# Gate projected channel by token, value sums and their denominators made in channel-by-token layout

## What is computed

```python
xn = layernorm(x)                                  # (16, 128, 64)
q, k, v = xn @ Wq, xn @ Wk, xn @ Wv                # 8 heads of 16 channels
attn = softmax(q @ k.T / 4)                        # per row and head, 128 x 128
out = (attn @ v) * sigmoid(xn @ Wg + bg)           # (16, 128, 128)
t = x + out @ Wo + bo
```

## Time and profile before

| | |
|---|---|
| median of 3 runs | 94.19 us (94.04 to 95.80) |
| the profiled execution | 94.28 us, of which the span of the profile is 92.5 us |
| TensorE | busy 75.1 us of the span (81%) |
| VectorE | busy 65.5 us (71%) |
| ScalarE | busy 63.1 us (68%) |
| GpSimd | busy 60.1 us (65%) |
| maxima, first and last row | start at 14.28 and 57.83 us |
| last row of `t_all` | starts at 66.84 us |
| granted TensorE clock | 0.969 of full speed, mean over the span |

### The profile page before, as it was taken

The page is one execution under the profiler, slowest core; times in us unless marked ns, Lnnn a source line. Parts: engine busy times, 40 slices in busy tenths (PEclk is TensorE's granted clock), DMA queues, the critical chain, the costliest instruction groups (busy, mean ns, idle before and its releaser), DMA issues.

```text
span 92.5 us, 2812 instructions
## 1 busy us (share of the span) xinstructions
PE 75.1 (81%) x928; PEld 51.3 (55%) x928; DVE 65.5 (71%) x246; ACT 63.1 (68%) x153; POOL 60.1 (65%) x112
## 2 busy tenths in 40 slices
PE   1988777699899999999999969898798949998000
PEld 1625444266575666566557556576586718997000
DVE  0657377865978887877797868845995576789850
ACT  4247649569979999999999957663335773578120
POOL 5851969841894764835899572647739576948950
PEclk9999999999999999999999999999999999999755
DMA  2768255567146426553355953000000000001103
GB/s 61 180 221 317 77 98 102 113 120 113 32 92 95 96 39 120 117 100 61 73 113 113 63 115 56 11 4 0 0 0 7 0 0 0 0 0 62 59 4 113
DMA packets 18862, 6.82 MB, mean 74 GB/s; under 512 B 17248, under 2 KB 18272, under 8 KB 18848
## 3 DMA queue, kind: packets, MB, share of 16 engines
q1 hardware_dynamic: 18480, 6.27, 33.1%
q10 hardware_dynamic: 368, 0.36, 1.6%
HBM read 1.91 MB, written 0.52 MB: 26 GB/s over the span
## 4 chain that ended last, share of the span: by engine, by line
PE 30%; DVE 19%; POOL 14%; issue 13%; ACT 13%; DMA 5%; DVEq 1%; POOLq 1%; ACTq 0%
PE bank L1045 5%; DMA qk_t<-stack 5%; DVE stack L531 5%; POOL rstd L943 4%; PE banks L1100 4%; PE banks L1105 3%; POOL stack L846 3%; ACT prob L364 3%; PE bank L1055 3%; ACT zn L452 2%; PE bank L1205 2%; PE bank L1019 2%; ACT stack L341 2%; PE banks L1004 2%; DVE xn L508 2%
## 5 line engine op out<-in xcount | busy, mean ns | idle before, releaser
L531 DVE TENSOR_REDUCE stack<-banks 128x8 f16<-128x1024 f32 x16 | 19.4, 1210 | 0.4 <-PE banks L1004 0.4
L364 ACT ACTIVATE prob<-banks 128x1024 f32<-128x1024 f32 x16 | 16.6, 1038 | 1.1 <-PE banks L1031 1.1
L846 POOL TENSOR_TENSOR stack<-qkg,stack 128x256 f16<-128x256 f32 x16 | 11.1, 694 | 8.4 <-ACT qkg L343 8.1
L856 POOL TENSOR_TENSOR og<-og,rden 128x128 f32<-128x128 f32 x16 | 6.4, 403 | 8.5 <-DVE og L549 8.5
L539 DVE COPY q_t<-bank 128x512 f16<-128x512 f16 x16 | 6.8, 424 | 7.3 <-PE bank L1019 7.3
L1045 PE MATMUL bank<-prob,v_aug 128*32 128x128 f32 x256 | 10.3, 279 | 0.6 <-ACT prob L364 0.6
L341 ACT ACTIVATE stack<-bank 128x512 f16<-128x512 f32 x16 | 9.6, 600 | 0.8 <-PE bank L993 0.8
L372 ACT ACTIVATE u_sb<-bank 128x256 f32<-128x256 f32 x16 | 6.3, 394 | 5.5 <-PE bank L1045 5.2
L784 POOL TENSOR_TENSOR rstd<-rstd,neg_half 128x4 f32<-128x4 f32 (+1 forms) x9 | 8.3, 920 | 0.8
L1105 PE MATMUL banks<-ones,ident 128*128 128x256 f16 x53 | 7.4, 273 | 1.5 <-DVE stack L531 1.5
L343 ACT ACTIVATE qkg<-bank 128x384 f32<-128x384 f32 x16 | 8.0, 500 | 0.0
(11 more groups left out here) (132 smaller groups left out, 185.6 us busy)
## 6 DMA issues: line engine op xcount, KB each, us to landing
w_in<-in_w SPq DMA_DIRECT2D x1, 512.0 KB, 5.6
out<-res SPq DMA_DIRECT2D x3, 128.0 KB, 1.9
x_all<-in_x SPq DMA_DIRECT2D x2, 128.0 KB, 2.5
x_all<-in_x SPq DMA_DIRECT2D x1, 256.0 KB, 3.2
w_in<-in_w SPq DMA_DIRECT2D x1, 256.0 KB, 5.8
b_b<-in_b SPq DMA_DIRECT2D x1, 256.0 KB, 6.0
qk_t<-stack SPq DMA_TRANSPOSE x16, 3.1
vectors_b<-in_vectors ACTq DMA_DIRECT2D x1, 160.0 KB, 3.5
```

What stands on the lines that cost most here:

```text
L364: nc.scalar.activation(prob[:, s % 2], s2_both_p, ACT.Exp, scale=HD ** -0.5).then_inc(exp_done, 1)
L531: nc.vector.tensor_reduce(q[:, :, :, SHIFT], s1_both_p, AX, ALU.max, negate=True).then_inc(max_done, 1)
L846: nc.gpsimd.tensor_tensor(stack_slots(b, 2, 0), qkg[:, b, 0:2 * INNER].rearrange("t (a h c) -> t a h c", a=2, h=HEADS), stack_slots(b, 0, ...
```

## The change

The value sums are no longer turned back to token by channel; everything up to Wo stays channel by token.

- **project** streams 384 columns (q, k, v) instead of 512, and two further matmuls hold the gate's 128 columns of w_hi and w_lo as weights and stream the row's tokens, so the gate comes out channel by token. ACT takes its tanh from PSUM with the bias (a column, halved once on DVE) as an operand. gate_input, gates and `gate` go.
- **values** sums two heads into the same 32 output channels: v_aug of the first holds [v, 0], of the second [0, v]. 8 more matmuls of the same shape with `twos` (2.0 or 0) as weights give each channel its denominator. Both outputs are 128 x 128.
- outputs, transpose_outputs, transpose_gated and gated go. gate_outputs reads both from PSUM: the reciprocal is now over 128 x 128 denominators. divide multiplies 128 x 128 by 128 x 128, and its output is project_out's weights.
- project_out and residual come one step earlier (OUT_LATE 6 to 5), STEPS is ROWS+6 instead of ROWS+9, and what follows on DVE, POOL and PE moves one step up. In the last steps PE runs shifted_scores ahead of values, and DVE runs copy_q ahead of gate_outputs.
- The turned q uses one bank throughout; the last row's values go to the projection's bank. Fillers shrink a little.

```diff
-Q_FREE = 13
-S1_LATE, Q_LATE, U_LATE, GATED_LATE, OUT_LATE = 2, 3, 4, 5, 6
-UT_LATE = 4
+STEPS = ROWS + 6
+
+
+S1_LATE, Q_LATE, U_LATE, OUT_LATE = 2, 3, 4, 5
...
-        u_p = bank[B_U][:, 0:2 * TOK].rearrange("c (a q) -> c a q", a=2)
-        ut_p = bank[B_UT][:, 0:2 * TOK].rearrange("q (h c) -> q h c", h=HEADS)
-        y_p = bank[B_U][:, 2 * TOK:2 * TOK + DIM]
+        u_p = [bank[b][:, 0:TOK] for b in (B_U, B_PROJ)]
+        den_p = [bank[b][:, TOK:2 * TOK] for b in (B_U, B_PROJ)]
+        y_p = bank[B_TURN][:, 0:DIM]
...
-                    act.wait_ge(gate_ok, s - 3)
                     act.wait_ge(tq2_done, s - 3)
-                qk = proj_p[:, 0:2 * INNER].rearrange("t (a h c) -> t a h c", a=2, h=HEADS)
-                nc.scalar.activation(stack_twice(b), qk.unsqueeze(3).broadcast_to([TOK, 2, HEADS, 2, HD]), ACT.Copy,
+                both = proj_p[:, 0:2 * INNER].rearrange("t (a h c) -> t a h c", a=2, h=HEADS)
+                nc.scalar.activation(stack_twice(b), both.unsqueeze(3).broadcast_to([TOK, 2, HEADS, 2, HD]), ACT.Copy,
                                      scale=1 / WSCALE)
-                nc.scalar.activation(qkg[:, b, :], proj_p[:, 0:3 * INNER], ACT.Copy,
-                                     scale=1 / WSCALE).then_inc(qkg_ok, 1)
+                nc.scalar.activation(qk[:, b, :], proj_p[:, 0:2 * INNER], ACT.Copy,
+                                     scale=1 / WSCALE).then_inc(qk_ok, 1)
                 if s >= V_BUFS:
                     act.wait_ge(pv_done, s - V_BUFS + 1)
-                nc.scalar.activation(v_aug[:, s % V_BUFS, :, 0:HD],
-                                     proj_p[:, 3 * INNER:4 * INNER].rearrange("t (h c) -> t h c", h=HEADS),
-                                     ACT.Copy, scale=1 / WSCALE).then_inc(proj_copied, 1)
-
-            def gates(s):
-
-                b = s % 4
-                act.wait_ge(gate_ok, s + 2)
-                if s >= 4:
-                    act.wait_ge(ut_read, s - 2)
-                nc.scalar.activation(th[:, b:b + 2, :], gate[:, b:b + 2, :], ACT.Tanh, scale=0.5).then_inc(tanh_done, 1)
+                nc.scalar.activation(value_slots(s % V_BUFS),
+                                     proj_p[:, 2 * INNER:3 * INNER].rearrange("t (p a c) -> t p a c", p=4, a=2),
+                                     ACT.Copy, scale=1 / WSCALE)
+                if s == 0:
+                    act.wait_ge(bg_ok, 1)
+                if s >= V_BUFS:
+                    act.wait_ge(u_read, s - V_BUFS + 1)
+                nc.scalar.activation(th[:, s % V_BUFS, :], proj_p[:, 3 * INNER:4 * INNER], ACT.Tanh, bias=bg_half[:, 0:1],
+                                     scale=0.5 / WSCALE).then_inc(proj_copied, 1)
...
-            def outputs(s):
-
-                b = s % 2
-                act.wait_ge(pv_done, s + 1)
-                if s >= 2:
-                    act.wait_ge(ut_done, s - 1)
-                nc.scalar.activation(u_sb[:, b], u_p, ACT.Copy).then_inc(u_copied, 1)
-
-            def gated(s):
-
-                b = s % 2
-                act.wait_ge(ogt_done, s + 1)
-                if s >= 2:
-                    act.wait_ge(wo_done, s - 1)
-                nc.scalar.activation(og_t[:, b, :], ogt_p, ACT.Copy).then_inc(ogt_copied, 1)
...
             def gate_outputs(s):
 
                 b = s % 4
-                dve.wait_ge(ut_done, s + 1)
-                dve.wait_ge(tanh_done, s // 2 + 1)
+                dve.wait_ge(pv_done, s + 1)
                 if s >= 4:
                     dve.wait_ge(og_ok, s - 3)
-                nc.vector.reciprocal(rden[:, b, :], ut_p[:, :, HD])
-                nc.vector.scalar_tensor_tensor(out=og1[:, b, :].rearrange("t (h c) -> t h c", h=HEADS),
-                                               in0=th[:, b, :].rearrange("t (h c) -> t h c", h=HEADS), scalar=1.0,
-                                               in1=ut_p[:, :, 0:HD], op0=ALU.add, op1=ALU.mult).then_inc(ut_read, 1)
+                nc.vector.reciprocal(rden[:, b, :], den_p[s // (ROWS - 1)])
+                dve.wait_ge(proj_copied, s + 1)
+                nc.vector.scalar_tensor_tensor(out=og1[:, b, :], in0=th[:, s % V_BUFS, :], scalar=1.0, in1=u_p[s // (ROWS - 1)],
+                                               op0=ALU.add, op1=ALU.mult).then_inc(u_read, 1)
...
+                if t >= ROWS+1 and live(t - S1_LATE):
+                    copy_q(t - S1_LATE)
+                if live(t - U_LATE):
+                    gate_outputs(t - U_LATE)
                 if live(t - OUT_LATE):
                     residual(t - OUT_LATE)
-                if live(t - S1_LATE):
+                if t < ROWS+1 and live(t - S1_LATE):
...
-            def gate_input(s):
+            def low(s):
+
                 b = s % 4
-                pool.wait_ge(qkg_ok, s + 1)
+                pool.wait_ge(qk_ok, s + 1)
+                nc.gpsimd.tensor_tensor(stack_slots(b, 2, 0),
+                                        qk[:, b, :].rearrange("t (a h c) -> t a h c", a=2, h=HEADS),
+                                        stack_slots(b, 0, 1), ALU.subtract).then_inc(split_ok, 1)
+
+            def divide(s):
+
+                b = s % 4
+                pool.wait_ge(u_read, s + 1)
                 if s >= 4:
-                    pool.wait_ge(tanh_done, (s - 4) // 2 + 1)
-                nc.gpsimd.tensor_tensor(gate[:, b, :], qkg[:, b, 2 * INNER:3 * INNER], bg_b, ALU.add).then_inc(gate_ok, 1)
...
+                nc.gpsimd.tensor_tensor(og[:, b, :], og1[:, b, :], rden[:, b, :], ALU.mult).then_inc(og_ok, 1)
...
-                nc.tensor.matmul(proj_p, x_t[:, s, :], w_hi[:, :], start=True, stop=False)
+                nc.tensor.matmul(proj_p[:, 0:3 * INNER], x_t[:, s, :], w_hi[:, 0:3 * INNER], start=True, stop=False)
                 if s == 0:
                     pe.wait_ge(w_lo_ok, 1)
-                nc.tensor.matmul(proj_p, x_t[:, s, :], w_lo[:, :], start=False, stop=True).then_inc(proj_done, 1)
+                nc.tensor.matmul(proj_p[:, 0:3 * INNER], x_t[:, s, :], w_lo[:, 0:3 * INNER], start=False, stop=True)
+                nc.tensor.matmul(proj_p[:, 3 * INNER:4 * INNER], w_hi[:, 3 * INNER:4 * INNER], x_t[:, s, :],
+                                 start=True, stop=False)
+                nc.tensor.matmul(proj_p[:, 3 * INNER:4 * INNER], w_lo[:, 3 * INNER:4 * INNER], x_t[:, s, :],
+                                 start=False, stop=True).then_inc(proj_done, 1)
...
-                drained("u", u_copied)
-                drained("y", t_ok)
+                if s == ROWS - 1:
+                    pe.wait_ge(proj_copied, ROWS)
+                else:
+                    drained("u", u_read)
+                if s == 0:
+                    pe.wait_ge(twos_ok, 3)
                 issued["u"] += 1
-                for a in range(2):
-                    for p in range(4):
-                        last = nc.tensor.matmul(u_p[32 * p:32 * p + 32, a, :], v_aug[:, b, 2 * p + a, :],
-                                                prob[:, s % 2, a, p, :], start=True, stop=True)
+                for what in range(2):
+                    target = (u_p, den_p)[what][s // (ROWS - 1)]
+                    for a in range(2):
+                        for p in range(4):
+                            columns = (v_aug[:, b, 2 * p + a, :], twos[:, VCOLS * a:VCOLS * (a + 1)])[what]
+                            last = nc.tensor.matmul(target[32 * p:32 * p + 32, :], columns, prob[:, s % 2, a, p, :],
+                                                    start=a == 0, stop=a == 1)
                 last.then_inc(pv_done, 1)
-
-            def transpose_outputs(s):
-                pe.wait_ge(u_copied, s + 1)
-                drained("turned", ut_read)
-                drained("q", tq2_copied)
-                issued["turned"] += 1
-                for a in range(2):
-                    last = nc.tensor.transpose(ut_p.rearrange("q (p a) c -> q p a c", a=2)[:, :, a, :],
-                                               u_sb[:, s % 2, a, :], ident[:, :])
-                last.then_inc(ut_done, 1)
-
-            def transpose_gated(s):
-                pe.wait_ge(og_ok, s + 1)
-                drained("gated", ogt_copied)
-                drained("x", x_t_ok)
-                issued["gated"] += 1
-                nc.tensor.transpose(ogt_p, og[:, s % 4, :], ident[:, :]).then_inc(ogt_done, 1)
 
             def project_out(s):
                 if s == 0:
                     pe.wait_ge(ld["columns"], 16)
-                pe.wait_ge(ogt_copied, s + 1)
-                drained("u", u_copied)
+                pe.wait_ge(og_ok, s + 1)
+                drained("x", x_t_ok)
                 drained("y", t_ok)
                 issued["y"] += 1
-                nc.tensor.matmul(y_p, og_t[:, s % 2, :], wo, start=True, stop=True).then_inc(wo_done, 1)
+                nc.tensor.matmul(y_p, og[:, s % 4, :], wo, start=True, stop=True).then_inc(wo_done, 1)
...
+                if t >= ROWS and live(t - Q_LATE):
```

(7 more changed lines are left out.)

144 lines of the change are left out of this document (63 added, 81 removed).

## The result

The changed kernel is slower. Its median is 100.72 us (99.59 to 101.07, four runs), beside 95.0 us for the kernel before on the same chip (94.04 to 96.21, four runs); the ratio is 1.068, with a 95% interval of 1.053 to 1.083. The ratio compares only the undisturbed executions of both kernels, so it is not the quotient of the two medians. The forecast was 97.4 us with a range of 95.0 to 100.0: the direction was right, the time lies outside the range, and the loss is 5.7 us where 3.2 were forecast (97.4 against the 94.19 shown).

A forecast was written before the change was run, and what follows sets the result against it. VectorE was to bind at 3.05 us a step. Start -0.7, middle +3.4 and tail +0.2 gave +2.9 on 94.28, so 97.2 us, put at 97.4 for small waits; range 95.0 to 100.0.

The forecast's parts named there:

- the middle: Stretch from row 3's maxima to row 15's, twelve steps: forecast 37.3 us against 33.94, +3.4.
- Behind it nothing is changed: From the last row of t_all to the end: no change in time, 0 us.
- VectorE becomes the bound: VectorE's step grows from 2.08 to 3.05 us, above TensorE's 2.79.
- I therefore take the upper slope: ... 1180 ns: VectorE's reciprocal of 128 elements: 8.1 ns an element on top of 206 ns for eight, 0.97 us more per row.
- PSUM costs nothing extra: Reading from PSUM instead of SBUF adds no time on VectorE: reduce from PSUM 167 ns, multiply from SBUF 172.
- rival 2: VectorE's reciprocal takes 0.9 to 1.05 us, VectorE and TensorE nearly level, total 93 to 96 us; chance 8%.
- So none in the middle: Between row 3's and row 15's maxima, no waits add to VectorE's step of 3.05 us.
- TensorE does not get shorter: TensorE's step: matmuls removed and added balance, 2.79 us before and after.
- Start, -0.7: Up to row 3's maxima: without gate_input of row 0 and with a narrower copy, 0.7 us sooner, at 23.2.
- Tail, +0.2: Row 15's maxima to the last row of t_all: 9.2 us against 9.0, three reciprocals eating the saved round.
- Rival 1: The reciprocal costs like any operation, 0.24 us, and TensorE binds at 2.79 us a step: 90.2 us; chance 13%.

The follow-up runs named there:

- experiment 2: The changed kernel with only 8 of the 128 denominators inverted on VectorE, every channel multiplied by one of these 8; 95.47 us, ratio 1.003 to the kernel before.
- experiment 4: The changed kernel with the copy of the turned q moved from VectorE to ScalarE, ahead of the row's exponential; 104.03 us, ratio 1.091 to the kernel before.
- experiment 6: The changed kernel with TensorE's turns of the inputs of rows 8 to 15 moved behind values, ScalarE's copies of them ahead of the exponential; 100.3 us.
- experiment 7: The changed kernel with 32 more matmuls on TensorE whose result nobody reads, in the last steps and behind the loop; 100.52 us.

## Why the prediction was right and wrong

In the profiled execution the loss was 6.7 us instead of 2.9. Of the 3.8 us more, 2.8 lie behind the tail, 0.6 in the start, 0.2 in the tail and 0.1 in the middle. The step that takes the time out of the range is therefore "Behind it nothing is changed"; the two errors in the middle nearly cancel.

- **VectorE becomes the bound: right.** It is busy 95% of the middle, TensorE 87%, ScalarE 69%; in experiment 2 nearly the whole loss goes with the reciprocal's size alone. Its load does not set the step by itself, though (experiment 4).
- **"I therefore take the upper slope: ... 1180 ns": wrong size.** 948 ns in the kernel, 894 alone. The term was 0.23 us a row too dear, 2.8 us in the middle and 0.7 in the tail. What failed here is "PSUM costs nothing extra", drawn from a reduce and a multiply: for a reciprocal of 8 it is 55 ns. Had only this been set right, the forecast would have been 97.4 - 3.5 = 93.9 us, no change at all; rival 2 priced exactly this reciprocal, at 93 to 96.
- **"So none in the middle": wrong.** 3.0 us of waits and stretched instructions lie there. The forecast looked at one wait alone (values for the gate, which indeed is only 0.2 us) and not at what stands behind the reciprocal in VectorE's order and who waits for that: the residual, the bank that it frees, the turn of the inputs, ScalarE's copy, the stack. Nor did it price that the change moves the output of project_out into the bank of that turn, and the turn behind scores. Of these 3.0 us the turn is 0.7 to 0.9 (experiment 6), the split beside GpSimd 0.5, and some 1.6 stay unassigned.
- **"TensorE does not get shorter", 2.79 us: nearly right.** Where TensorE binds, in experiment 2, three steps are 2.69 to 2.70 us with TensorE busy all of them. Sixteen more instructions cost 0.46 us (forecast 0.48), the gate's two matmuls 0.06 each (0.08).
- **Start, -0.7: wrong.** It was -0.06. Without the gate's 0.60 us on GpSimd the same scaling of the inputs waits for VectorE's own moments, and the inputs landed 0.85 us later in this execution.
- **Tail, +0.2: it was +0.44**, but by another sum. Three reciprocals cost 0.7 less than forecast, so about 0.9 us of waits were missing. The largest part is the last row's way from its gate over GpSimd and TensorE to the residual: 1.23 us (69.53 to 70.76) against the 0.85 of the sum. The rest is spread over the wait for copy_q, the way to row 14's values and its moments, 0.1 to 0.2 us each.
- **"Behind it nothing is changed": wrong, +2.78 us.** The instructions are the same, but TensorE ran the first ten microseconds of them at half its clock. In experiment 7 the clock stayed full and the stretch took 25.98 us. In most executions of the new layout it costs less, about 1.7 us (27.2 to 27.5 against 25.66). The forecast took the clock behind the tail for given; what makes it fall stays open.
- **Rival 1 (90.2 us with a cheap reciprocal): wrong by its own test**, experiment 2, 95.47. Its middle was 1.8 us too short, its tail 0.8, and it had no clock.

That the sum reached the right sign is partly luck: an over-priced reciprocal stood in for waits that it had left out.

## What to carry to other kernels

When an operation on an engine grows, price the ring that it lies on and not only the engine's sum: the same long reciprocal cost 2.5 us of the twelve steps in one layout (37.48 - 34.97) and 8.3 in the other (42.24 - 33.94), since in the latter a shared bank tied it to 2.28 us of TensorE's work. When an output moves to another bank, ask who else uses that bank and who queues behind them. A stretch whose instructions do not change can still change its time: look at the granted clock there, in several executions, since here neither TensorE's busy share ahead of it (93% in experiment 2) nor the layout told for certain whether it would fall. And two rows that differ in two ways (count and memory) give no slope.
